# Attention block kernel: kept index weights, no table of factors, and the low parts of absorbed query weights on GpSimd from one staging buffer

## The chip, the cores and the metric

The kernel runs on one core of a Trainium2 chip. The metric is the time of one execution on the device in microseconds (us), as the median over runs. PE is TensorE, ACT is ScalarE, DVE is VectorE, POOL is GpSimd, SP is SyncE, whose queue issues every DMA of this kernel.

## The reference

One transformer block over 1024 rows of 512 numbers. With `xn = layernorm(x)` the result is `x + attention(xn) + experts(xn)`.

```python
q_lat = rmsnorm(xn @ q_a_w); q = q_lat @ q_b_w        # 32 heads, 128 + 64 rotated columns
ckv = xn @ kv_a_w                                      # 64 latent + 64 rotated key columns
kv = rmsnorm(kv_lat) @ kv_b_w                          # keys (128) and values (128) of each head
scores = (q_nope . k_nope + rope(q_pe) . rope(k_pe)) * 192 ** -0.5
iq = (xn @ idx_wq_w)                                   # 16 index heads of 128 columns
idx_scores = sum_n iw[n] * relu(iq[n] . ik)            # a score of each query for each key
mask = top 128 keys of idx_scores, and causal
out = softmax(where(mask, scores, -inf)) @ v @ o_w     # then + low-rank experts, top 2 of 8
```

The choice of the top 128 keys needs nearly full precision, so the kernel splits each float32 operand in a high half in float16 and a low half (the float32 value less the high half, in float16) and takes three products: high-high, high-low, low-high.

## The kernel before

All of the work is one hand-ordered program: each engine has its own list of instructions, and semaphores tie them together. There is no planner; the order of each list is the order of the code.

**Opening** (to about 46 us). Layer norm, transposes of the rows to `xnT` and one projection of 472 columns.

**Index scores, first group** (to about 112 us, `GROUPS[0]`, row tiles 3, 2, 1). For each of 16 index heads `n`, PE's `iq_head(n)` (line 567) multiplies the index weight of that head with `xnT` for rows 128 to 511, and `idx_head` (line 583) multiplies the result with the index keys. The weight comes in float32 by DMA (`load_iq`, line 376) into one of two slots of `wq32`. ACT's `weights` (line 856) copies it to float16 and scales the float32 copy, and POOL's `wq_parts` (line 1364, subtraction at line 1366) makes the low half. Both halves land in one of two slots of `wqp`.

**Index scores, second group** (to about 191 us, `GROUPS[1]`, row tiles 5 and 4; iterations `n` = 0 to 15). PE needs the index queries of rows 512 to 1023, so `iq_head(16 + n)` (matmuls through `indexer`, line 558) wants the same 16 weights again: they are loaded, copied and split a second time, two heads ahead. ACT takes the relu of each bank (line 899) and weighs it (line 876), POOL sums it into `bias` (`join`, line 1432), and DVE meanwhile picks the top 128 of the first group, eight at a time (`top_round`, lines 1182 and 1189). In iterations 3 to 12 PE also transposes normalised rows (line 604), which ACT and DVE copy out. DVE's masks (line 1199) end the group.

**Index scores, third group, and absorbed query weights** (to about 283 us, `GROUPS[2]`, row tiles 7 and 6). In iteration `n` PE does tiles 7 and 6 and `qw_pair(n)` (line 607, matmuls at 614): the product of the latent query weights and the key weights of two heads, 256 columns in `psT`. ACT's list is: relu and weighing of tile 7, relu of tile 6, then four copies of 128 columns to float16 (two from `pe_s`, the rotated columns, two from `psT`, the latent ones; lines 968 to 971) and a scaled copy of `pe_s` in place (line 973). The low halves are split between two engines. DVE makes those of the latent columns straight from PSUM (lines 1221 and 1222), after a top-8 round and the sum of tile 6 (line 1133). POOL makes those of the rotated columns from `pe_s` (`pe_low`, lines 1486 to 1492), after its sum of tile 7. SP loads the operands of pair `p` in three DMAs (`load_qw`, line 391) once both low halves of pair `p - 2` are made. Query units 0 and 1 are also computed, rotated and stored in this stage: after iterations 4 and 9 POOL rotates (`rope_cos`, `rope_sin`, lines 1445 to 1458), and in iterations 6, 8, 12 and 13 it makes one low half each (`q_low`, `rope_low`).

**Attention** (to about 787 us). 32 units (two heads, half of the rows) of 8 steps. A step is scores on PE, row minimum on DVE (line 1242), exponential on ACT, transposes by PE or DMA, the float16 split, and the product with the values. `unit_out` (line 1255) closes a unit on DVE: reciprocal of the row sums, a product of the eight reciprocals with the table `scaled` (line 1260; 1024 for the steps transposed by DMA, 1 for the others), and one multiplication of the whole bank (line 1265).

**Output** (to the end). 48 matmuls a row tile from weights kept in SBUF (line 779), and the rows are stored.

```python
for n in range(IH):                              # DVE, third group
    top_round(GROUPS[1])
    acc(psS[1], 6, n, 3 * IH + n, 5 * IH + 2 * n + 1, 1 if n else 0)
    u = n % 2
    dve.wait_ge(qw_hi, 4 * n + 4)
```

## Time and profile before

| what | value |
|---|---|
| median of 3 runs | 883.79 us (880.57 to 884.02) |
| the profiled execution | 884.29 us |
| its span in the profile | 882.5 us |
| PE busy | 792.2 us, 90% of the span |
| DVE busy | 659.0 us, 75% |
| ACT busy | 583.1 us, 66% |
| POOL busy | 580.6 us, 66% |
| share of the chain that ended last | PE 29%, POOL 26%, DVE 15%, issue 13% |

How to read it: an engine's busy time is a mean over stages that have different limits, so no single share says what bounds the kernel. The span is the time between the first and the last instruction in the profile; the execution's own time is longer by 1.8 us. The chain of waits follows the last instruction back to what released it, step by step.

### The profile page before, as it was taken

Reading aid. Unit: us, or ns where it says so; the run is one execution under the profiler, and the core shown is the slowest. Engines: PE = TensorE matmul, PEld = TensorE weight load, DVE = VectorE, ACT = ScalarE, POOL = GpSimd, SP = SyncE. Lnnn points to the kernel's source line nnn. Section 1 sums busy time; section 2 is a strip of 40 time slices with the busy share of each in tenths; the row PEclk is TensorE's granted clock in tenths of the full one; section 3 lists DMA queues with packets and bytes.
Section 4 is the critical chain, followed back from the end, with each engine's and each line's share of the span. In section 5 each row is a group of like instructions: output and inputs, shape, how many; then the busy total and the mean of one; then the engine's idle time right before and its main releaser. Section 6 shows DMA issues by size and latency. Waiting matters only on the chain.

```text
span 882.5 us, 20077 instructions
## 1 busy us (share of the span) xinstructions
PE 792.2 (90%) x7384; PEld 487.0 (55%) x7384; DVE 659.0 (75%) x1557; ACT 583.1 (66%) x1308; POOL 580.6 (66%) x509
## 2 busy tenths in 40 slices
PE   4979989977776998888888999999999999999998
PEld 2545544434443555555554677776766776764443
DVE  6365677889999999999988888888887888851000
ACT  2656789988886887877877677666666676750000
POOL 3175368876795788878877787887788888740000
PEclk9989999999999999999999999999999999999999
DMA  8012211112343776666676567897777677871110
GB/s 258 25 37 72 72 49 48 49 53 64 109 123 98 153 170 164 174 168 159 169 164 151 111 128 141 154 157 147 138 137 152 131 152 153 165 152 34 52 53 29
DMA packets 198483, 104.00 MB, mean 118 GB/s; under 512 B 146417, under 2 KB 172401, under 8 KB 198385
## 3 DMA queue, kind: packets, MB, share of 16 engines
q1 hardware_dynamic: 198384, 102.72, 51.9%
q8 instruction: 59, 0.97, 0.5%
q14 instruction: 40, 0.32, 0.1%
HBM read 36.62 MB, written 6.29 MB: 49 GB/s over the span
## 4 chain that ended last, share of the span: by engine, by line
PE 29%; POOL 26%; DVE 15%; issue 13%; DMA 7%; SPq 6%; ACT 4%; POOLq 0%; DVEq 0%; ACTq 0%
PE psS L779 9%; DMA arena<-arena 6%; DVE m L1182 4%; SPq L457 4%; PE psS L706 3%; DVE bias L1189 3%; POOL arena L1457 3%; POOL arena L1455 3%; POOL arena L1483 3%; PE psT L578 2%; PE psS L535 2%; DVE arena L1242 2%; PE psT L558 2%; POOL arena L1366 2%; POOL arena L1462 2%
## 5 line engine op out<-in xcount | busy, mean ns | idle before, releaser
L706 PE MATMUL psS<-keyT,arena 128*128 128x512 f16 (+3 forms) x1152 | 231.5, 329 | 14.9 <-DVE small L1242 6.6
L810 ACT ACTIVATE arena<-psT 128x512 f16<-128x512 f32 (+4 forms) x328 | 154.6, 503 | 110.7 <-PE psT L763 65.8
L1242 DVE CUSTOM_DVE_ANT_0 arena<-psS,bias 128x512 f32<-128x512 f32 (+7 forms) x256 | 191.4, 751 | 41.3 <-PE psS L706 17.6
L997 ACT ACTIVATE arena<-arena,small 128x512 f32<-128x512 f32 (+7 forms) x256 | 197.4, 774 | 27.7 <-DVE small L1242 21.1
L1048 DVE SCALAR_TENSOR_TENSOR arena<-psT,arena 128x512 f16<-128x512 f32 (+3 forms) x246 | 126.3, 535 | 23.1 <-ACT arena L810 22.8
L706 PEld LDWEIGHTS psS<-keyT,arena 128*128 128x128 f16 x1152 | 92.6, 98 | 81.2 <-issue 20.7
L591 PE MATMUL psS<-ikT,big 128*128 128x512 f16 (+3 forms) x528 | 103.8, 341 | 24.2 <-DVE bias L1133 20.8
L1432 POOL TENSOR_TENSOR bias<-arena,bias 128x768 f32<-128x768 f32 (+2 forms) x48 | 91.3, 1916 | 32.3 <-ACT arena L876 21.4
L763 PE MATMUL psT<-ident,arena 128*128 128x128 f32 x624 | 97.0, 277 | 10.1 <-DVE arena L1048 6.9
L591 PEld LDWEIGHTS psS<-ikT,big 128*128 128x128 f16 x528 | 49.5, 100 | 73.8 <-DVE bias L1133 28.1
L1189 DVE MATCH_REPLACE8 bias<-m,bias 128x768 f32<-128x768 f32 (+4 forms) x112 | 89.9, 809 | 0.0
L763 PEld LDWEIGHTS psT<-ident,arena 128*128 128x128 f32 x624 | 72.6, 141 | 29.5 <-ACT arena L997 13.8
L1182 DVE MAX8 m<-bias 128x8 f32<-128x768 f32 (+4 forms) x112 | 87.4, 816 | 0.5
L810 ACT ACTIVATE big<-psT 128x512 f16<-128x512 f32 (+1 forms) x64 | 36.3, 568 | 59.5 <-PE psT L742 31.9
L733 PEld LDWEIGHTS psO<-val,arena 128*128 128x128 f16 x1728 | 66.2, 99 | 11.9 <-issue 1.7
L1366 POOL TENSOR_TENSOR arena<-arena 128x512 f16<-128x512 f32 x32 | 37.1, 1161 | 53.9 <-ACT arena L810 53.8
L733 PE MATMUL psO<-val,arena 128*128 128x64 f16 x1728 | 69.5, 194 | 0.5 <-DVE arena L1048 0.2
L1048 DVE SCALAR_TENSOR_TENSOR big<-psT,big 128x512 f16<-128x512 f32 (+1 forms) x64 | 41.9, 655 | 34.4 <-ACT big L810 34.0
L810 ACT ACTIVATE arena<-arena 128x512 f16<-128x512 f32 (+1 forms) x112 | 62.7, 590 | 0.8 <-DMA arena<-in_wiq 0.7
L1455 POOL TENSOR_TENSOR arena<-arena,sq 128x512 f32<-128x512 f32 x32 | 40.8, 1275 | 33.8 <-DMA arena<-arena 33.8
L1483 POOL TENSOR_TENSOR arena<-arena 128x512 f16<-128x512 f32 (+4 forms) x37 | 55.3, 1496 | 3.0
L1133 DVE SCALAR_TENSOR_TENSOR bias<-psS,arena,bias 128x512 f32<-128x512 f32 (+3 forms) x64 | 45.1, 746 | 16.3 <-ACT psS L899 15.8
(164 smaller groups left out, 1417.0 us busy)
## 6 DMA issues: line engine op xcount, KB each, us to landing
arena<-arena SPq DMA_DIRECT2D x192, 128.0 KB, 2.4
arena<-in_wiq SPq DMA_DIRECT2D x32, 256.0 KB, 2.8
arena<-in_ow SPq DMA_DIRECT2D x16, 512.0 KB, 4.1
arena<-in_qbT SPq DMA_DIRECT2D x16, 256.0 KB, 2.5
wvo_parts<-arena SPq DMA_DIRECT2D x16, 256.0 KB, 2.0
arena<-in_qpe SPq DMA_DIRECT2D x16, 128.0 KB, 3.0
arena<-in_x SPq DMA_DIRECT2D x8, 256.0 KB, 3.2
out<-arena SPq DMA_DIRECT2D x8, 256.0 KB, 2.0
```

Of the source, the lines that this page charges most:

```text
L591: last = mm(bank[:, c:c + w], iq[:, a, n, t * P:(t + 1) * P], ikT[:, b, c:c + w], start=(a, b) == (0, 0), stop=(a, b) == (1, 0))
L706: last = mm(bank[:, k:k + w], Q[:, u % 2, h, a, q:q + P], keyT[:, b, h, k:k + w], start=(a, b) == (0, 0), stop=(a, b) == (1, 0))
L733: last = mm(dst, src[:, a, j * P:(j + 1) * P], val[:, b, j, :], start=j == 0 and n == 0, stop=j == nb - 1 and n == 2)
L763: last = nc.tensor.transpose(bank[:, (j % 4) * P:(j % 4 + 1) * P], pr[:, g % 4, j * P:(j + 1) * P], ident[:])
L810: return nc.scalar.activation(dst, src, ACT.Copy, scale=scale)
L997: nc.scalar.activation(pr[:, g % 4, 0:kw], pr[:, g % 4, 0:kw], ACT.Exp, bias=shift[:, g % 4:g % 4 + 1], scale=-1.0, accum_out=rsum[:, unit ...
L1048: return v.scalar_tensor_tensor(out=dst, in0=src, scalar=scale, in1=hi, op0=ALU.mult, op1=ALU.subtract)
L1182: v.max(m8[:, slot], bias[:, TOFF[t]:TOFF[t + 1]]).then_inc(tk_max, 1)
L1189: v.match_replace(out=row, in_to_replace=m8[:, slot], in_values=row, imm_value=TAKEN).then_inc(tk_rep, 1)
L1242: v.tensor_tensor_reduce(out=pr[:, g % 4, 0:kw], in0=bank[:, 0:kw], in1=bias[:, TOFF[t]:TOFF[t + 1]], scale=-c_s, scalar=3e38, op0=ALU.add ...
L1432: g.tensor_tensor(row, src[:, 0:P * (t + 1)], row, ALU.add).then_inc(sum_done, 1)
L1483: g.tensor_tensor(rows_of_turn(d)[:, kw:2 * kw], pr[:, x % 4, 0:kw], rows_of_turn(d)[:, 0:kw], ALU.subtract).then_inc(row_lo, 1)
```

## The change

- **Kept index weights.** `wqp` becomes 16 homes, one for each index head, laid into memory that is free until the third group: `cq` and `sq` (the cosine and sine tables, 4 homes), the arena (5), `w1lo` (4) and `w2s` (3). The second pass of loads, ACT copies and POOL subtractions is gone, and so is PE's wait for it. The tables are loaded after head 19, the first query weights after head 24.
- **No table of factors.** The `scaled` table and its product are gone. `unit_out` multiplies in three instructions in the lower half of the rows and in two in the upper; the one that takes steps transposed by DMA carries the factor 1024.
- **One staging buffer.** `pe_s` gives way to `both`, 256 columns for each of the two operands of a pair: rotated (loaded by DMA, scaled in place) and latent (copied by ACT out of `psT`). ACT then makes each high half in one copy of 256 columns, and POOL's `w_low` each low half in one subtraction of 256 columns. DVE makes none. ACT waits for POOL's low halves of pair `n - 2` before it writes the buffer; PE waits for ACT's copy out of `psT` instead of for DVE.

```diff
-        wqp = view(o + 1024, 4 * HID, F16).rearrange("p (u s k n) -> p u s k n", u=2, s=2, k=KT)
+        wq_homes = ([t[:].bitcast(F16) for t in (cq, sq)] + [view(15488, 3 * 2 * HID, F16), view(o + 1024, 4 * HID, F16)]
+                    + [t[:].rearrange("p a b -> p (a b)") for t in (w1lo, w2s)])
+        wqp = []
+        for home, slots in zip(wq_homes, (2, 2, 3, 2, 4, 3)):
+            wqp += [home[:, 1024 * j:1024 * (j + 1)].rearrange("p (s k n) -> p s k n", s=2, k=KT) for j in range(slots)]
...
-        pe_s = view(15040 + 1280, 2 * 256).rearrange("p (u k n) -> p u k n", u=2, k=2)
+        both = view(16000, 2 * 512).rearrange("p (u k n) -> p u k n", u=2, k=2)
...
-            for i in range(0, IH // 2):
-                load_iq(2 * i, 0, IH, False)
-                load_iq(2 * i + 1, 1, IH, False)
+            sp.wait_ge(iq_mm, IH + 4)
             sp.dma_start(cq[:], cosq).then_inc(ld_cq, 16)
             sp.dma_start(sq[:], sinq).then_inc(ld_cq, 16)
+            sp.wait_ge(iq_mm, IH + 9)
...
             def load_qw(p, u, first):
                 if not first:
-                    sp.wait_ge(qw_lo, 2 * p - 2)
                     sp.wait_ge(pe_lo, 2 * p - 2)
...
             def iq_head(q):
-                u, c = q % 2, q // IH
-                pe.wait_ge(wq_lo, q + 1)
+                u, (c, n) = q % 2, divmod(q, IH)
+                if not c:
+                    pe.wait_ge(wq_lo, n + 1)
...
                 if p >= 2:
-                    pe.wait_ge(qw_lo, 2 * p - 2)
+                    pe.wait_ge(st_sc, 2 * p - 3)
...
-                if q + 2 < 2 * IH:
+                if q + 2 < IH:
                     weights(q + 2, u, False)
...
-                copy(w1hi[:, n, 0:128], pe_s[:, u, 0, :], WQ_S).then_inc(qw_hi, 1)
-                copy(w2s[:, n, 0:128], pe_s[:, u, 1, :], WQ_S).then_inc(qw_hi, 1)
-                copy(w1hi[:, n, 128:256], psT[u][:, 0:128], WQ_S).then_inc(qw_hi, 1)
-                copy(w2s[:, n, 128:256], psT[u][:, 128:256], WQ_S).then_inc(qw_hi, 1)
-                act.wait_ge(qw_hi, 4 * n + 2)
-                copy(pe_s[:, u], pe_s[:, u], WQ_S).then_inc(pe_sc, 1)
+                if n >= 2:
+                    act.wait_ge(pe_lo, 2 * n - 2)
+                copy(both[:, u, :, 128:256], psT[u][:, 0:256].rearrange("p (k n) -> p k n", k=2), WQ_S).then_inc(st_sc, 1)
+                copy(both[:, u, :, 0:128], both[:, u, :, 0:128], WQ_S).then_inc(st_sc, 1)
+                act.wait_ge(st_sc, 2 * n + 2)
+                copy(w1hi[:, n, :], both[:, u, 0, :], 1.0).then_inc(qw_hi, 1)
+                copy(w2s[:, n, :], both[:, u, 1, :], 1.0).then_inc(qw_hi, 1)
...
                 acc(psS[1], 6, n, 3 * IH + n, 5 * IH + 2 * n + 1, 1 if n else 0)
-                u = n % 2
-                dve.wait_ge(qw_hi, 4 * n + 4)
-                low(w1lo[:, n, 128:256], psT[u][:, 0:128], WQ_S, w1hi[:, n, 128:256]).then_inc(qw_lo, 1)
-                low(w2s[64:128, n, 128:256], psT[u][64:128, 128:256], WQ_S, w2s[64:128, n, 128:256]).then_inc(qw_lo, 1)
...
-                dve.wait_ge(ri_done, 2 * u + 1)
-                v.tensor_tensor(rinv, rinv, scaled[:, u // NP], ALU.mult).then_inc(ri_done, 1)
...
-                v.tensor_tensor(op.rearrange("p k (h r) -> p h k r", h=2),
-                                out_bank(u).rearrange("p (h k r) -> p h k r", h=2, k=4),
-                                rinv.rearrange("p (h k) -> p h k", h=2).unsqueeze(3).broadcast_to([P, 2, 4, KVR]),
-                                ALU.mult).then_inc(o_done, 1)
+                step = 4 // len(TURNED[u // NP])
+                v.tensor_tensor(to[:, 0], bank[:, 0], by[:, 0].unsqueeze(2).broadcast_to([P, 4, KVR]), ALU.mult)
+                if step == 2:
+                    v.tensor_tensor(to[:, 1, 1::2], bank[:, 1, 1::2], by[:, 1, 1::2].unsqueeze(2).broadcast_to([P, 2, KVR]), ALU.mult)
+                v.scalar_tensor_tensor(out=to[:, 1, 0::step], in0=bank[:, 1, 0::step], scalar=PR_S,
+                                       in1=by[:, 1, 0::step].unsqueeze(2).broadcast_to([P, 4 // step, KVR]),
+                                       op0=ALU.mult, op1=ALU.mult).then_inc(o_done, 1)
...
-                if IH + n + 2 < 2 * IH:
-                    wq_parts(IH + n + 2, n % 2)
...
-            def pe_low(n):
-                pool.wait_ge(pe_sc, n + 1)
-                g.tensor_tensor(w1lo[:, n, 0:128], pe_s[:, n % 2, 0, :], w1hi[:, n, 0:128], ALU.subtract).then_inc(pe_lo, 1)
+            def w_low(n):
+                pool.wait_ge(qw_hi, 2 * n + 1)
+                g.tensor_tensor(w1lo[:, n, :], both[:, n % 2, 0, :], w1hi[:, n, :], ALU.subtract).then_inc(pe_lo, 1)
+                pool.wait_ge(qw_hi, 2 * n + 2)
                 pool.wait_ge(pe_lo, 2 * n + 1)
-                g.tensor_tensor(w2s[64:128, n, 0:128], pe_s[64:128, n % 2, 1, :], w2s[64:128, n, 0:128],
+                g.tensor_tensor(w2s[64:128, n, :], both[64:128, n % 2, 1, :], w2s[64:128, n, :],
                                 ALU.subtract).then_inc(pe_lo, 1)
```

## Rows read from the trace of the kernel before

**Rows 1.** Windows: stretch, length, busy time of each engine, clock, DMA share, GB/s.
```profile
131.00:191.00 60.00, 55.11 (x310) 28.53 (x309) 47.20 (x122) 55.88 (x86) 50.52 (x34) 1.00 0.19 55
200.00:278.00 78.00, 57.24 (x326) 32.44 (x325) 76.61 (x138) 67.69 (x130) 60.33 (x57) 1.00 0.36 104
340.00:470.00 130.00, 113.61 (x1169) 71.68 (x1167) 122.08 (x350) 104.14 (x297) 103.75 (x102) 0.97 0.68 166
490.00:780.00 290.00, 286.18 (x3739) 203.58 (x3738) 240.46 (x529) 202.65 (x421) 231.96 (x181) 1.00 0.76 145
```
**Rows 2.** Chain of waits, second group: start, us, what.
```profile
164.74 1.17 POOL arena L1366
```
**Rows 3.** Order of time, PE: start, us, line, shapes, count, idle before and releaser.
```profile
112.20 2.75 PE L558 MATMUL psT<-arena 128*128 128x512 f16 x12
...
165.95 2.76 PE L558 MATMUL psT<-arena 128*128 128x512 f16 x12 [0.40 <-POOL arena L1366]
...
170.34 0.61 PE L604 MATMUL psO<-ident,arena 128*128 128x128 f32 x4
...
187.42 2.76 PE L558 MATMUL psT<-arena 128*128 128x512 f16 x12 [0.98 <-POOL arena L1366]
...
237.11 1.00 PE L614 MATMUL psT<-arena 128*128 128x64 f32 x8
```
**Rows 4.** Order of time, ACT, second group.
```profile
163.85 1.14 ACT L810 ACTIVATE arena<-arena 128x512 f16<-128x512 f32 x2
```
**Rows 5.** Order of time, DVE, third group, first and last iterations.
```profile
200.64 1.67 DVE L1182 MAX8 m<-bias 128x8 f32<-128x768 f32 x2
...
276.94 0.28 DVE L1048 SCALAR_TENSOR_TENSOR w1lo<-psT,w1hi 128x128 f16<-128x128 f32 x1
...
277.58 1.69 DVE L1182 MAX8 m<-bias 128x8 f32<-128x768 f32 x2
```
**Rows 6.** Order of time, ACT, third group, iterations 7 and 8.
```profile
238.15 0.31 ACT L810 ACTIVATE w1hi<-arena 128x128 f16<-128x128 f32 x1
...
238.88 0.41 ACT L810 ACTIVATE arena<-arena 128x256 f32<-128x256 f32 x1
...
242.69 0.90 ACT L899 ACTIVATE psS<-psS 128x896 f32<-128x896 f32 x1
```
**Rows 7.** Order of time, POOL, third group, iterations 4 to 6.
```profile
224.97 1.27 POOL L1450 TENSOR_TENSOR arena<-arena,cq 128x512 f32<-128x512 f32 x1
...
228.90 2.36 POOL L1432 TENSOR_TENSOR bias<-arena,bias 128x1024 f32<-128x1024 f32 x1
231.21 0.43 POOL L1488 TENSOR_TENSOR w1lo<-arena,w1hi 128x128 f16<-128x128 f32 x1
231.72 0.42 POOL L1490 TENSOR_TENSOR w2s<-arena,w2s 64x128 f16<-64x128 f32 x1
...
235.54 1.16 POOL L1466 TENSOR_TENSOR arena<-arena 128x512 f16<-128x512 f32 x1
```
**Rows 8.** Order of time, SP's queue, one load of query weights.
```profile
251.88 0.33 SPq L395 DMA_DIRECT2D arena<-in_qbT  x1
...
252.73 0.59 SPq L397 DMA_DIRECT2D arena<-in_qpe  x1
```
**Rows 9.** The page's DMA issues: count, KB each, median us to landing.
```profile
arena<-in_qpe SPq DMA_DIRECT2D x16, 128.0 KB, 3.0
```
**Rows 10.** Line 379 (loads of index weights), all 32.
```profile
DMA to landing us min/median/max: 2.6/2.8/6.3
```
**Rows 11.** Groups by line and shape, DVE, 110 to 205 us: count, busy, mean ns.
```profile
L1199 DVE TENSOR_SCALAR bias<-bias 128x384 f32<-128x384 f32 x1 | 1.7, 1690 | 0.0
...
L1199 DVE TENSOR_SCALAR bias<-bias 128x256 f32<-128x256 f32 x1 | 0.3, 278 | 0.0
```
**Rows 12.** Order of time, DVE, the close of a unit.
```profile
654.40 0.17 DVE L1260 TENSOR_TENSOR small<-small 128x8 f32<-128x8 f32 x1
654.65 0.69 DVE L1265 TENSOR_TENSOR arena<-psO,small 128x512 f32<-128x512 f32 x1
```

More of the change, by code:

```diff
@@ L180, in block_kernel @@
         eps_t = small[:, 400:401]
-        scaled = small[:, 408:424].rearrange("p (c s) -> p c s", c=2)
         nmax_s = small[:, 424:428]
@@ L369, in _, with load_iq @@
             sp.dma_start(bm32, bm).then_inc(ld_c, 16)
+            wiq_v = wiq.rearrange("(k p) n -> p k n", p=P)
+            def load_iq(n, u, first):
+                if not first:
+                    sp.wait_ge(wq_lo, n - 1)
+                sp.dma_start(wq32[:, u], wiq_v[:, :, ds(n * ID, ID)]).then_inc(ld_wq[u], 16)
+            load_iq(0, 0, True)
+            load_iq(1, 1, True)
+            for n in range(2, IH):
+                load_iq(n, n % 2, False)
+            sp.wait_ge(iq_mm, IH + 4)
             sp.dma_start(cq[:], cosq).then_inc(ld_cq, 16)
             sp.dma_start(sq[:], sinq).then_inc(ld_cq, 16)
-            wiq_v = wiq.rearrange("(k p) n -> p k n", p=P)
-            def load_iq(n, u, again, first):
-                if not first:
-                    sp.wait_ge(wq_lo, n + again - 1)
-                sp.dma_start(wq32[:, u], wiq_v[:, :, ds(n * ID, ID)]).then_inc(ld_wq[u], 16)
-            load_iq(0, 0, 0, True)
-            load_iq(1, 1, 0, True)
-            for i in range(1, IH // 2):
-                load_iq(2 * i, 0, 0, False)
-                load_iq(2 * i + 1, 1, 0, False)
-            for i in range(0, IH // 2):
-                load_iq(2 * i, 0, IH, False)
-                load_iq(2 * i + 1, 1, IH, False)
+            sp.wait_ge(iq_mm, IH + 9)
             def load_qw(p, u, first):
                 if not first:
-                    sp.wait_ge(qw_lo, 2 * p - 2)
                     sp.wait_ge(pe_lo, 2 * p - 2)
@@ L396, in load_qw @@
                 sp.dma_start(wk_s[:, u], wkT[:, ds(2 * p, 2), :]).then_inc(ld_qw[u], 16)
-                sp.dma_start(pe_s[:, u].rearrange("p k (h r) -> p k h r", h=2),
+                sp.dma_start(both[:, u, :, 0:128].rearrange("p k (h r) -> p k h r", h=2),
                              qpe[:, :, ds(2 * p, 2), :]).then_inc(ld_qw[u], 16)
@@ L577, in iq_head @@
                     for a, b in ((0, 0), (0, 1), (1, 0)):
-                        last = mm(psT[u][:, 0:CH - P], wqp[:, u, a, k, :], xnT[:, b, k, P:CH],
+                        last = mm(psT[u][:, 0:CH - P], wqp[n][:, a, k, :], xnT[:, b, k, P:CH],
                                   start=ins == 0, stop=ins == 3 * KT - 1)
@@ L1258, in unit_out @@
                 v.reciprocal(rinv, rsum[:, u % 2, :]).then_inc(ri_done, 1)
-                dve.wait_ge(ri_done, 2 * u + 1)
-                v.tensor_tensor(rinv, rinv, scaled[:, u // NP], ALU.mult).then_inc(ri_done, 1)
                 dve.wait_ge(av_mm, UNIT_AV[u])
-                dve.wait_ge(ri_done, 2 * u + 2)
+                dve.wait_ge(ri_done, u + 1)
                 if u:
                     dve.wait_ge(ot_mm, u)
-                v.tensor_tensor(op.rearrange("p k (h r) -> p h k r", h=2),
-                                out_bank(u).rearrange("p (h k r) -> p h k r", h=2, k=4),
-                                rinv.rearrange("p (h k) -> p h k", h=2).unsqueeze(3).broadcast_to([P, 2, 4, KVR]),
-                                ALU.mult).then_inc(o_done, 1)
+                to = op.rearrange("p k (h r) -> p h k r", h=2)
+                bank = out_bank(u).rearrange("p (h k r) -> p h k r", h=2, k=4)
+                by = rinv.rearrange("p (h k) -> p h k", h=2)
+                step = 4 // len(TURNED[u // NP])
[5 more added lines that the diff above has]
+                                       op0=ALU.mult, op1=ALU.mult).then_inc(o_done, 1)
             def ot_low(bank, u):
@@ L1347, in _ @@
             g.memset(eps_t, EPS).then_inc(eps_ok, 1)
-            g.memset(small[:, 408:424], 1.0).then_inc(ones_ok, 1)
-            pool.wait_ge(ones_ok, 1)
-            for c in range(2):
-                for s in TURNED[c]:
-                    at = col_of(s)
-                    ins = g.memset(scaled[:, c, at:at + 1], PR_S)
-            ins.then_inc(eps_ok, 1)
             g.memset(bias[:], 0.0).then_inc(idx_init, 1)
@@ L1421, in _ @@
             gated_rows()
-            for q in range(6, IH + 2):
+            for q in range(6, IH):
                 wq_parts(q, q % 2)
```

23 lines of the change are left out of this document (10 added, 13 removed).

## The prediction

> **What bounds the kernel now.** I read the windows first, to see which engine is full in which stretch, then the chain of waits inside a stretch to see what its end hangs on, then the order of time of one engine for the durations. Four stretches matter [rows 1]. From 131 to 191 us (index heads of row tiles 5 and 4, call it stage D) PE is busy 55.1 of 60 us and ACT 55.9. From 200 to 278 us (tiles 7 and 6, with the absorbed query weights beside them, stage E) DVE is busy 76.6 of 78. In attention, DVE has 122.1 of 130 us in the lower half and PE 286.2 of 290 in the upper.
>
> In stage D the chain steps from GpSimd's subtraction of line 1366, the low part of a reloaded index weight, straight into the head's matmuls [rows 2], and PE shows it as idle time before the head, 0.40 us in a typical iteration [rows 3]. That is the last link of a loop: load, two ACT copies, subtraction, matmul. The two ACT copies alone take 1.14 us [rows 4] on an engine that is otherwise full.
>
> In stage E the DVE iterations follow one another without a gap: the first two maxima start at 200.64 and the sixteenth at 277.58 [rows 5], 76.94 us for 15 iterations, 5.13 each. The loop is rigid because nothing but DVE's own list sets it. Its last 0.64 us of 5.13 (276.94 to 277.58) are the two low parts of lines 1221 and 1222.
>
> **Part 1, kept index weights.** In stage D the change removes 16 loads, 32 ACT copies, 16 POOL subtractions, and PE's wait for them. After that PE has only its own work: from the start of a head to the start of the transposes 4.39 us (165.95 to 170.34), and the transposes take 0.61 us with pipelining, of which I count 0.5 [rows 3]. So 4.89 us in the ten iterations with transposes and 4.39 in the others. From the head that starts at 112.20 to the last one there are 14 steps, ten with transposes and four without: 48.9 + 17.6 = 66.5 us, so the last head starts at 178.7 and not at 187.42. **Gain 8.7 us.** Could another engine take PE's place? ACT falls from about 5.3 us an iteration by 1.14 to some 4.2, POOL from 4.5 to 3.3, DVE has 47.2 busy of 60 us, 4.2 an iteration [rows 1]. All are below 4.89, and below 4.39 by less, so the gain holds, with DVE and ACT next. The tail from the last head to DVE's first maximum of stage E (187.42 to 200.64) is DVE's own two rounds and masks beside POOL's last sums, and moves along whole. Bounds: if ACT or DVE hold every iteration to 5.1 us, 14 x 5.1 = 71.4 gives 3.8; PE's idle time all gone, 9.5.
>
> The moved DMAs: the cosine and sine tables go from the opening to the middle of stage D, where the share of the DMA engines is 0.19 [rows 1]; the first reader is the rotation at 225 us [rows 7], 80 us later. The first loads of query weights wait for head 25, which is also long before stage E. I cost both at nothing; the cover is those tens of us.
>
> **Part 2, the low parts on GpSimd.** DVE loses 0.64 us of each iteration: 16 x 0.64 = 10.2 us, if everyone else can follow a period of 4.50. Here the others come close.
>
> ACT: its small copies and the scaling run from 238.15 to 239.29, 1.14 us [rows 6]. After it are four copies of 128x256; one lasts 0.41 and lets the next start after about 0.3, and the third must wait for the end of the second: 0.3 + 0.4 + 0.05 + 0.3 + 0.3 = 1.35 us. With 2.95 us of other work ACT needs 4.3 of 4.5.
>
> POOL: a sum of 1024 columns occupies it 2.31 us (228.90 to 231.21), a 128x128 low part 0.43 with 0.08 to the next (231.21 to 231.72), a 128x512 one 1.16 [rows 7]. No row shows 128x256; the line between 0.43 and 1.16 gives 0.67, the bounds are 0.43 (as if width were free) and 0.9. I take 0.67, since both neighbours are this same operation. An iteration is then 2.31 + 2 x 0.75 = 3.81 us. On top come two rotations of 3.93 us each (224.97 to 228.90) after iterations 4 and 9, and four subtractions of about 1.12 in iterations 6, 8, 12 and 13: 12.3 us. Sixteen times 3.81 plus 12.3 is 73.3 us, against 16 x 4.50 = 72.0 for DVE. POOL is full, and late after each rotation.
>
> Who waits when POOL is late? One staging buffer (two slots) is freed by POOL alone, and the next-but-one load on SP waits for it. From its low part to the next-but-one copies: three DMAs, the last issued 0.85 us after the first (251.88 to 252.73) and landing 3.0 us later [rows 8, 9], then 1.00 us of PE for the products (row at 237.11) [rows 3], 4.9 us in all. Walk the first rotation in the times of before, stage E still beginning at 200.64. The sum of iteration 4 starts near 202.7 + 4 x 4.5 = 220.7; with its low parts it ends at 224.5, the rotation at 228.5, iteration 5 with its low parts at 232.3. The copies of iteration 7 can start at 237.3, and from the copies of 7 to the relu of iteration 8 ACT needs 4.54 us (238.15 to 242.69) [rows 6]. That relu ends near 242.7, where DVE wants it at 240.4. **2.3 us lost.** The second rotation repeats the pattern with POOL already behind: 2.6 us. Twice more, where ACT also empties a query bank, 0.4. Loss 5.7, so stage E saves 10.2 - 5.7 = **4.5 us**.
>
> GpSimd's low parts were off the chain in iterations; they are 16 x 0.5 us more now. The Trainium skill, "GPSIMD Engine Reference", section 4.1 "Engine selection", speaks against this part: elementwise work with two inputs is about twice as slow there as on VectorE and belongs on VectorE. The rows agree in kind (0.43 against about 0.3 us for 128x128), but by that rule alone one would forecast a loss, while by rows the receiving engine had 18 us idle [rows 1].
>
> The end of stage E: the two masks of tiles 5 and 4 begin while POOL is in its last low parts, which before had ended first. In stage D's tail a mask of 384 columns that overlapped POOL's sums lasted 1.69 us, the one of 256 after them 0.28 [rows 11]. I charge **0.5 us** (bounds 0 and 1.5). The Trainium skill, "SBUF — State Buffer", section "SBUF: two separate sides", states that such a VectorE operation and a GpSimd one hold a shared port exclusively for a whole instruction. This trace agrees; by that rule the charge would reach the 1.5.
>
> **Part 3, no table of factors.** Per unit DVE loses the small product and the wait behind it, 0.25 us (654.40 to 654.65) [rows 12]. The multiplication, 0.69 us, becomes three instructions in the lower half and two in the upper; each further one costs fixed time: the line through 0.28 us for a low part of 128 columns [rows 5] and 0.69 for 512 has 0.14 of it, of which about half overlaps the neighbour, 0.07. Net -0.11 x 16 in the lower half, where DVE is nearly full, and -0.18 x 16 where PE is the bound [rows 1] and it is worth nothing. At most 1.8, and a loss of 0.5 if nothing overlaps; I take **1.0 us**. The memsets at the start lie beside the projections: nothing.
>
> **Sum.** 8.7 + 4.5 - 0.5 + 1.0 = 13.7 us off the profiled execution's 884.29 (span 882.5 and 1.8 around it) gives 870.6. That execution stands 0.5 above the median 883.79, so a median of **870.1 us**. Its own range, by the bounds above, is 866 to 874.
>
> **Rivals.**
> *A. POOL keeps up*, because the 128x256 low part is near 0.5 or loads land faster. Then stage E saves the whole 10.2: 870.1 - 5.7 = 864.4 us. For it: POOL idle 18 us in the stage. Against: the rotations are lumps, and slack before them can't be banked.
> *B. POOL becomes the bound outright.* At 0.9 us a low part an iteration takes 4.27 and the stage 68.3 + 12.3 = 80.6, which with its late start ends where it ends now. Stage E saves 0 to 1: 874 us.
> *C. Stage D gives half*, held by ACT or DVE at 5.1 us an iteration: 870.1 + 4.9 = 875 us. Against: their sums above.
> *D. Nothing to measure*, both stages finding new waits: 882 us, within 0.5%, which is about what a measurement of this kernel tells from no change.
> *E. Slower.* The place is the ring from one low part over SP's load and PE's products to the next-but-one low part: 4.9 + 1.35 + 1.5 = 7.75 us for two iterations, against 9.0. It holds while loads land in 3 us. Were they to land in 6.3 us, the longest landing of an index weight [rows 10], the ring is 11.05, or 5.5 an iteration; sixteen are 88.4, and with POOL's 12.3 lying inside, 100.7 us against 82.1 now: 870.1 + 4.5 + 18.6 = 893 us. It decides from landings of about 5.7 us on. Against: the median of 3.0 in this stage.
>
> **How the numbers follow.** Forecast 0.57, A 0.12, B 0.14, C 0.08, D 0.05, E 0.04. The likeliest gives 870.1. The range takes in A's 864.4 and C's 875 with their own spread, 863 to 878, and leaves out D, E and a little. Faster by over 0.5% (below 879.4): forecast, A, B and C, 0.91. Within: 0.05. Slower: 0.04.
>
> **What would show it.** Stage D: PE's heads 4.9 us apart with no idle time before them, no line 1366 in the chain; a gap of 5.1 or more speaks for C. Stage E: DVE's maxima 4.5 us apart except for two gaps of 6.5 to 7.3 us, near iterations 8 and 13; sixteen even gaps of 4.5 mean A, even gaps near 5 mean B, and PE idle before the products after SP's loads in every iteration E. The 128x256 low part on GpSimd at 0.67 us. Attention unchanged but for about 1 us in the lower half. The forecast is wrong if stage D ends less than 6 us earlier, or stage E takes over 80 or under 73 us.

## The result, and the profile after

The change makes the kernel faster, by less than forecast: 875.42 us as the median of five runs (874.79 to 876.89) against 883.79 (880.57 to 886.68), a ratio of 0.992 with an interval of 0.989 to 0.995. The forecast was 870.1, with a range of 863 to 878.

The profiled execution took 874.79 us, with a span of 872.9. Four marks cut the span: DVE's first maximum of stage E, the first row minimum of attention, and PE's first final product.

| stretch | before, us | after, us | difference | predicted |
|---|---|---|---|---|
| to the first maximum of stage E | 200.64 | 191.20 | -9.44 | -8.7 |
| stage E, to the first row minimum | 83.07 | 83.88 | +0.81 | -4.5 + 0.5 |
| attention, to the final products | 503.16 | 501.95 | -1.21 | -1.0 |
| final products to the end | 95.63 | 95.87 | +0.24 | 0 |

So the whole gain stands in stage D, and the staging buffer, which takes 0.64 us of work off DVE sixteen times, brought nothing. That is what the experiments had to explain.

The page's busy times of the kernel after, and what its chain consists of:

```profile
PE 792.2 (91%) x7384; PEld 487.7 (56%) x7384; DVE 645.0 (74%) x1541; ACT 570.0 (65%) x1260; POOL 569.6 (65%) x486
...
PE 40%; DVE 4%; issue 1%; ACT 0%; DVEq 0%
```

Windows of the kernel after (stretch, length, busy time of PE, PE's weight loads, DVE, ACT and POOL, granted clock, DMA share, GB/s):

```profile
131.00:181.00 50.00, 50.00 (x289) 27.16 (x287) 44.84 (x117) 44.07 (x63) 34.86 (x21) 1.00 0.07 19
191.00:273.00 82.00, 63.56 (x334) 35.35 (x332) 70.44 (x114) 71.26 (x120) 68.51 (x56) 0.93 0.34 99
216.00:222.00 6.00, 4.70 (x26) 2.39 (x24) 5.35 (x9) 5.93 (x11) 5.84 (x5) 1.00 0.27 76
226.60:236.00 9.40, 9.33 (x39) 5.35 (x39) 3.80 (x7) 5.32 (x9) 5.42 (x6) 0.68 0.47 128
256.00:262.00 6.00, 5.93 (x29) 3.80 (x30) 2.76 (x6) 3.66 (x7) 4.85 (x4) 0.72 0.37 99
```

In stage D (131 to 181) PE is busy all of the 50 us; nothing else is near. In stage E (191 to 273) DVE is busy 70.4 of 82 us, where it had been busy 76.6 of 78 [rows 1]: its list is shorter and it now waits. And the granted clock of the whole stage is 0.93 where it was 1.00. Two short stretches carry that fall, 0.68 and 0.72. In them PE is busy nearly all the time and DVE less than half of it. In the 6 us before the first of them (216 to 222) ACT and POOL are busy 5.93 and 5.84 us: there both are full.

Stage D in order of time, PE (start, us, line, shapes, count):

```profile
163.96 2.75 PE L558 MATMUL psT<-arena,w1lo 128*128 128x512 f16 x12
...
168.34 0.61 PE L605 MATMUL psT<-ident,arena 128*128 128x128 f32 x4
168.78 2.75 PE L558 MATMUL psT<-arena,w2s 128*128 128x512 f16 x12
...
177.99 2.75 PE L558 MATMUL psT<-arena,w2s 128*128 128x512 f16 x12
```

The heads are 4.82 us apart (163.96 to 168.78) and no idle time stands before them, where 0.40 and 0.98 stood before [rows 3]. The last head starts at 177.99 instead of 187.42.

Stage E in order of time, DVE (start, us, line, shapes, count, idle before and releaser):

```profile
222.65 1.68 DVE L1182 MAX8 m<-bias 128x8 f32<-128x768 f32 x2
227.01 1.68 DVE L1182 MAX8 m<-bias 128x8 f32<-128x768 f32 x2
236.21 1.15 DVE L1133 SCALAR_TENSOR_TENSOR bias<-psS,arena,bias 128x896 f32<-128x896 f32 x1 [5.81 <-ACT psS L898]
237.28 1.68 DVE L1182 MAX8 m<-bias 128x8 f32<-128x768 f32 x2
...
263.28 1.15 DVE L1133 SCALAR_TENSOR_TENSOR bias<-psS,arena,bias 128x896 f32<-128x896 f32 x1 [4.52 <-ACT psS L898]
```

A normal iteration is 4.36 to 4.37 us (222.65 to 227.01), not 5.13 as in [rows 5]. The next one is 10.27 (227.01 to 237.28), because DVE stands idle 5.81 us before the sum of tile 6. The same happens five iterations on. Over all 15 gaps between maxima the gain is 15 x (5.13 - 4.37) = 11.4 us. Against 4.37 each, the two long gaps give back 5.9 and 4.6 us, three small ones (5.11, 4.99, 4.51) another 1.5. That is 12.0 us, and 77.52 us from first to last maximum instead of 76.94.

DVE names ACT as its releaser. ACT waited for PE's products, and PE's rows tell the rest. First POOL and SP (start, us), then PE:

```profile
217.73 1.27 POOL L1447 TENSOR_TENSOR arena<-arena 128x512 f32<-128x512 f32 x1
219.09 2.36 POOL L1424 TENSOR_TENSOR bias<-arena,bias 128x1024 f32<-128x1024 f32 x1
221.41 0.67 POOL L1478 TENSOR_TENSOR w1lo<-arena,w1hi 128x256 f16<-128x256 f32 x1
222.22 0.67 POOL L1481 TENSOR_TENSOR w2s<-arena,w2s 64x256 f16<-64x256 f32 x1
...
222.92 0.33 SPq L396 DMA_DIRECT2D arena<-in_qbT  x1
...
223.76 0.59 SPq L398 DMA_DIRECT2D arena<-in_qpe  x1
```

```profile
226.67 1.97 PE L615 MATMUL psT<-arena 128*128 128x64 f32 x8 [2.58 <-DMA arena<-in_qpe]
228.43 0.63 PE L624 MATMUL psT<-qlT,w1hi 128*128 128x512 f16 x1
228.86 0.63 PE L625 MATMUL psT<-qlT,w1hi 128*128 128x512 f16 x1
...
230.57 3.64 PE L592 MATMUL psS<-ikT,big 128*128 128x512 f16 x12
234.04 1.00 PE L615 MATMUL psT<-arena 128*128 128x64 f32 x8
...
256.07 1.54 PE L615 MATMUL psT<-arena 128*128 128x64 f32 x8 [3.62 <-DMA arena<-in_qpe]
```

Read it as a relay. POOL's rotation ends at 219.0, its late sum and low parts of pair 5 at 222.89. SP issues the load of pair 7 at 222.92, and the products of pair 7 start at 226.67, after 2.58 us of idle PE. Then comes what the prediction didn't have: the products last 1.97 us where they last 1.00 otherwise (234.04), the 512-column matmuls are 0.43 us apart (228.43 to 228.86), and the clock of the stretch is 0.68. PE has fallen from 2.4 to 1.2 GHz after the idle time, and is back at full speed at about 234 (products of 1.00 us). The Trainium skill, "TensorE: Matmul & The Clock Gate", section "HAM oscillation — how this bites in real kernels", tells of a kernel in which a wait for a DMA drops the clock, so that the work behind the wait starts cold. The rows above agree.

**The theory of load ring and clock:** the staging buffer's gain is given back in two waits of PE for a load that POOL's late low parts release, and a part of each loss, about 2 us, is the clock behind the wait. **The rival of full engines:** POOL or ACT is simply full, and any version with these low parts on POOL takes as long. **The rival of a disturbance:** the shorter stage D or the new memory places disturb stage E, and the buffer alone would gain. For the small term there is the question whether the missing table is worth anything.

### The profile page after: what moved, and what is told of

Same layout as the page of the kernel before. It is cut to its first block and busy times, and to the rows that moved or that the text cites. A ratio compares the mean times of both kernels' runs of the same rounds, so it can differ in the third digit from the quotient of the medians.

```text
span 872.9 us, 19970 instructions
## 1 busy us (share of the span) xinstructions
PE 792.2 (91%) x7384; PEld 487.7 (56%) x7384; DVE 645.0 (74%) x1541; ACT 570.0 (65%) x1260; POOL 569.6 (65%) x486
## 5 line engine op out<-in xcount | busy, mean ns | idle before, releaser
L809 ACT ACTIVATE arena<-psT 128x512 f16<-128x512 f32 (+5 forms) x344 | 160.3, 496 | 114.6 <-PE psT L762 62.7
L1473 POOL TENSOR_TENSOR ikT<-arena,ikT 128x384 f16<-128x384 f32 (+4 forms) x37 | 51.9, 1403 | 3.0
```

Source lines behind the costliest of these rows:

```text
L809: return nc.scalar.activation(dst, src, ACT.Copy, scale=scale)
L1473: g.tensor_tensor(rows_of_turn(d)[:, kw:2 * kw], pr[:, x % 4, 0:kw], rows_of_turn(d)[:, 0:kw], ALU.subtract).then_inc(row_lo, 1)
```

## The experiments

Each run was compared with the kernel before on the same chip, whose own median was 883.0 to 885.0 us; between two runs of small difference the ratio says more than the median. "Stage E" is the time from its first maximum to the first row minimum.

| run | median, us | ratio to before (interval) | first maximum | stage E | to final products | two long gaps |
|---|---|---|---|---|---|---|
| the change | 875.42 | 0.992 (0.989 to 0.995) | 191.20 | 83.88 | 501.95 | 10.27, 8.98 |
| keep_only | 874.54 | 0.989 (0.986 to 0.992) | 190.79 | 83.26 | 500.99 | none |
| stage_only | 885.28 | 1.001 (0.999 to 1.003) | 200.86 | 85.38 | 501.92 | 11.19, 9.60 |
| table_only | 882.85 | 0.998 (0.997 to 1.000) | 200.21 | 83.16 | 501.83 | none |
| fill | 871.80 | 0.985 (0.983 to 0.987) | 191.09 | 81.14 | 499.61 | 8.18, 7.98 |
| three_slots | 869.41 | 0.983 (0.980 to 0.987) | 190.23 | 78.09 | 501.99 | none |
| early_load | 869.16 | 0.983 (0.981 to 0.985) | 190.93 | 80.33 | 500.12 | 6.18, 8.56 |
| early_fill | 869.15 | 0.984 (0.982 to 0.986) | 191.00 | 81.03 | 499.84 | 7.91, 6.99 |
| split_rope | 871.18 | 0.985 (0.983 to 0.986) | 191.25 | 80.87 | 501.48 | 6.22, 9.06 |
| late_low | 869.32 | 0.982 (0.979 to 0.984) | 191.17 | 76.60 | 506.47 | none |
| defer_low | 869.98 | 0.985 (0.983 to 0.986) | 191.41 | 76.51 | 503.36 | none |

The columns behind the ratio are of one profiled execution each, whose own time can lie a few us from its median.

### One part alone

**keep_only** is the kernel after with the old staging and the old table: the kept index weights alone.

```diff
-                copy(both[:, u, :, 128:256], psT[u][:, 0:256].rearrange("p (k n) -> p k n", k=2), WQ_S).then_inc(st_sc, 1)
...
+                copy(w1hi[:, n, 0:128], pe_s[:, u, 0, :], WQ_S).then_inc(qw_hi, 1)
...
+                low(w1lo[:, n, 128:256], psT[u][:, 0:128], WQ_S, w1hi[:, n, 128:256]).then_inc(qw_lo, 1)
+                low(w2s[64:128, n, 128:256], psT[u][64:128, 128:256], WQ_S, w2s[64:128, n, 128:256]).then_inc(qw_lo, 1)
```

> Kept index weights alone: the staging buffer and the split multiplication undone. Theory (the second group gave 9.4 us of the 9.8, the third group nothing): the span falls from 882.5 to 872.5 to 874, the second group's heads stand 4.82 us apart, and the third group takes 82 us with DVE's period at 5.13. Rival (the staging buffer gave its 4.5 us and something else lost them): the span stays above 876.

**stage_only** is the reverse: only the staging buffer, with the second pass of index weights and the table as before. The buffer lies on the index weights' memory, so the first load of query weights waits for the last index head.

```diff
+            sp.wait_ge(iq_mm, 2 * IH)
...
-                if q + 2 < IH:
+                if q + 2 < 2 * IH:
                     weights(q + 2, u, False)
```

> Staging buffer alone: weights reloaded and the table kept; the first loads of query weights start only once the last index head is done, since the memory overlaps. Theory: the third group still takes 81 to 83 us against 82.1, with two long gaps in DVE (about 5.8 and 4.5 us, PE's granted clock below 0.8 after each), and the time is within 1.5 us of before. Rival (the two gaps come from the other parts, the loads of the tables among them): no gaps, 72 to 78 us, some 4 to 8 us faster.

keep_only alone has all of the change's gain: stage E starts at 190.79 and its maxima are 5.13 to 5.14 apart behind the first gap of 5.00, as before the change. Its span, 870.6 us, lies below the 872.5 to 874 expected, because its attention is shorter too (500.99). stage_only has no gain: ratio 1.001. Its maxima are 4.37 apart but for two gaps of 11.19 and 9.60, and 5.11 and 5.03. The clock from 191 to 273 us is 0.90. Here is PE before the first of the two:

```profile
237.64 1.97 PE L613 MATMUL psT<-arena 128*128 128x64 f32 x8 [3.90 <-DMA arena<-in_qpe]
```

The waits and the fall come with the buffer and without the kept weights, so the rival of a disturbance is out.

**table_only** is the kernel before without the table: at the end of a unit, three multiplications (lower half) or two (upper half) instead of one.

```diff
-                dve.wait_ge(ri_done, 2 * u + 1)
-                v.tensor_tensor(rinv, rinv, scaled[:, u // NP], ALU.mult).then_inc(ri_done, 1)
...
+                v.tensor_tensor(to[:, 0], bank[:, 0], by[:, 0].unsqueeze(2).broadcast_to([P, 4, KVR]), ALU.mult)
```

> The table of factors gone and the multiplication split, all else as before. Theory (what the prediction took): 0.11 us a unit in the lower half, 0 to 2 us faster in all, the upper half of attention unchanged; a unit's close on DVE 0.11 us shorter in the lower half and 0.18 in the upper. Rival (it does nothing, and the 1.2 us by which attention was shorter after the change is scatter of attention itself): within 0.5 us, though the close of a unit is shorter.

It is 1.5 us faster (884.38 to 882.85), a ratio of 0.998 (0.997 to 1.000), and attention is 1.3 us shorter in the profile. The close of a unit on DVE, from the reciprocal to the next work, falls from 1.12 us (393.67 to 394.79) to 1.02 (391.56 to 392.58) in the lower half and from 1.09 (654.17 to 655.26) to 0.95 (653.37 to 654.32) in the upper, against 0.11 and 0.18 expected. So the close is shorter, and the term of 1.0 us fits. That the whole time gains nothing isn't excluded by much: the interval ends at 0.9999, and keep_only, which has the table, had a shorter attention still (500.99).

### The load ring and the clock

**fill** is the kernel after with matmuls that nobody reads (22 ahead of PE's wait for pair 7, 30 ahead of that for pair 12), in a part of the bank that is free then. It adds work to PE and takes none of the waits away.

```diff
-                pe.wait_ge(ld_qw[u], 48 * (p // 2) + 48)
...
+                for _ in range({7: 22, 12: 30}.get(p, 0)):
+                    mm(psT[u][:, 256:512], qlT[:, 0, 0:128], qlT[:, 1, 0:256], start=True, stop=True)
+                pe.wait_ge(ld_qw[u], 48 * (p // 2) + 48)
```

> The changed kernel with 22 and 30 matmuls of 256 columns whose result nobody reads, placed on PE just before its waits for the loads of pairs 7 and 12. Theory (each gap is a wait for a load of 2.6 to 3.6 us, and then about 2.5 us more because PE runs at half speed after it): granted clock stays at 1.00 after both waits, the gaps in DVE fall from 5.8 and 4.5 us to about 3.3 and 2.3, the third group from 81.9 to some 77, the time by 4 to 5 us. Rival (GpSimd is full and sets the length; PE's clock only fills time that it would wait anyway): third group within 1 us of 81.9.

PE in order of time, and the window that had a clock of 0.68:

```profile
223.83 2.57 PE L613 MATMUL psT<-qlT 128*128 128x256 f16 x22
...
227.41 1.10 PE L617 MATMUL psT<-arena 128*128 128x64 f32 x8 [1.01 <-DMA arena<-in_qpe]
...
229.43 2.59 PE L592 MATMUL psS<-ikT,big 128*128 128x512 f16 x12
```

```profile
226.60:236.00 9.40, 7.51 (x43) 4.39 (x44) 5.67 (x10) 7.35 (x14) 7.53 (x7) 1.00 0.46 133
```

Added work makes the kernel 3.6 us faster (875.42 to 871.80), somewhat less than the 4 to 5 us expected; measured each against its own runs of the kernel before, the change gains 8.4 us and fill 13.2. PE still waits for the load and its products even start 0.74 us later (227.41 against 226.67), but they take 1.10 us and not 1.97, and the twelve head matmuls 2.59 and not 3.64. The gaps shrink by 2.1 and 1.0 us, and stage E by 2.7. This is the clock's part of the loss, less what the later start costs; the rest of the gap is the wait itself.

**three_slots** gives the staging buffer a third slot and lets SP load the other operands as soon as PE has read the pair before last, so that POOL may be a whole iteration late.

```diff
-        both = view(16000, 2 * 512).rearrange("p (u k n) -> p u k n", u=2, k=2)
+        both = [view(at, 512).rearrange("p (k n) -> p k n", k=2) for at in (16000, 16512, 13312)]
...
-                    sp.wait_ge(pe_lo, 2 * p - 2)
+                    sp.wait_ge(qw_mm, p - 1)
...
+                if p >= 3:
+                    sp.wait_ge(pe_lo, 2 * p - 4)
...
-                if n >= 2:
-                    act.wait_ge(pe_lo, 2 * n - 2)
+                if n >= 3:
+                    act.wait_ge(pe_lo, 2 * n - 4)
```

> The changed kernel with three slots of the staging buffer in place of two, and the loads of the query and key weights started when PE has read the pair before the last, not when GpSimd has made its low parts. GpSimd's work is the same. Theory (the loads come late because a slot waits for GpSimd): PE no longer waits for a load, its clock stays near 1.00, the third group takes 74 to 77 us and the time falls by 5 to 7 us. Rival (GpSimd's own 73 us with what it must wait for set the length): 80 us or more, less than 2 us gained.

Both long gaps are gone. The longest is 5.41, and from the first to the last maximum it is 69.1 us (190.23 to 259.34). The time falls as expected (6.0 us, expected 5 to 7), the stage a little less (78.1, expected 74 to 77). The rival of full engines fails in its strong form: with the same work on POOL and ACT the stage is 5.8 us shorter. But POOL takes over at the end. The last maxima and masks are early, and then DVE waits for POOL's last sum:

```profile
263.70 1.43 DVE L1202 TENSOR_SCALAR bias<-bias 128x768 f32<-128x768 f32 x2
268.32 0.69 DVE L1241 CUSTOM_DVE_ANT_0 arena<-psS,bias 128x512 f32<-128x512 f32 x1 [3.19 <-POOL bias L1427]
```

Behind it PE waits for POOL's last low part (waits of the same kernel from 260 to 300: engine and line, releaser, us in total, times, longest):

```profile
PE psS L708 <- POOL w2s L1484: 4.1, 1, 4.1
```

And behind this wait the clock falls: from 268 to 274 us it is 0.72 here, where early_load (below) has 1.00. The third slot took the falls out of the stage and left one at the start of attention:

```profile
268.00:274.00 6.00, 4.43 (x20) 2.61 (x21) 3.97 (x12) 3.00 (x8) 3.14 (x5) 0.72 0.35 100
```

**early_load** keeps two slots. Only the last of the three DMAs, the one into the staging buffer, still waits for POOL; the other two go once PE has read the pair before last.

```diff
-                    sp.wait_ge(pe_lo, 2 * p - 2)
+                    sp.wait_ge(qw_mm, p - 1)
...
+                if not first:
+                    sp.wait_ge(pe_lo, 2 * p - 2)
                 sp.dma_start(both[:, u, :, 0:128].rearrange("p k (h r) -> p k h r", h=2),
```

> The changed kernel, still two slots; the loads of query and key weights start when PE has read the pair before the last, and only the rotated columns wait for GpSimd's low parts. Theory (a load's way is issue of the two others, 0.85 us, and landing, 3.0; the ring through GpSimd stays): both waits of PE shorten by about 0.85 us but PE's clock still falls after them, the two gaps in DVE go from 5.8 and 4.5 us idle to about 4.6 and 3.4, the third group from 83.9 (first maximum to first row minimum) to 81 to 82. Rival (the order of the loads, not the number of slots, was what three slots repaired): the group falls to below 77.

That takes SP's two earlier issues off the ring, and PE's first wait shrinks from 2.58 to 1.41 us; the second is 2.75. PE in order of time:

```profile
226.17 1.10 PE L617 MATMUL psT<-arena 128*128 128x64 f32 x8 [1.41 <-DMA arena<-in_qpe]
227.11 0.38 PE L626 MATMUL psT<-qlT,w1hi 128*128 128x512 f16 x1
...
228.19 2.59 PE L594 MATMUL psS<-ikT,big 128*128 128x512 f16 x12
...
251.77 1.97 PE L617 MATMUL psT<-arena 128*128 128x64 f32 x8 [2.75 <-DMA arena<-in_qpe]
253.53 4.82 PE L594 MATMUL psS<-ikT,big 128*128 128x512 f16 x12
```

After 1.41 us of idle the clock stayed and the gap is 6.18; after 2.75 it fell, and the gap is 8.56. A fall behind both had been expected; with only one the stage is 80.3 us, below the 81 to 82 expected.

**early_fill** adds 24 unread matmuls to early_load, ahead of the wait for pair 12 alone.

```diff
+                for _ in range({7: 0, 12: 24}.get(p, 0)):
+                    mm(psT[u][:, 256:512], qlT[:, 0, 0:128], qlT[:, 1, 0:256], start=True, stop=True)
```

> The kernel with the earlier loads, plus 24 matmuls of 256 columns whose result nobody reads, on PE just before its wait for the load of pair 12, where PE stood idle 2.75 us and its clock fell. The load itself is untouched. Theory (the fallen clock is a cost of its own beside the wait): granted clock 1.00 after that wait, DVE's gap there 8.56 us from maximum to maximum before, 6.2 to 6.8 now; the other gap (6.18) stays. Rival (the wait alone makes the gap): 8.3 us or more.

At pair 12 the gap goes from 8.56 to 6.99 (6.2 to 6.8 expected) with the clock at 1.00, another 1.6 us of clock. But at pair 7, where the two kernels do the same, this execution fell. PE in order of time, then a window of each kernel, early_fill first:

```profile
226.32 1.08 PE L619 MATMUL psT<-arena 128*128 128x64 f32 x8 [1.48 <-DMA arena<-in_qpe]
227.24 0.49 PE L628 MATMUL psT<-qlT,w1hi 128*128 128x512 f16 x1
227.52 0.63 PE L629 MATMUL psT<-qlT,w1hi 128*128 128x512 f16 x1
...
229.23 3.37 PE L594 MATMUL psS<-ikT,big 128*128 128x512 f16 x12
```

```profile
224.00:240.00 16.00, 12.69 (x64) 6.64 (x62) 12.55 (x21) 13.23 (x23) 14.01 (x12) 0.89 0.42 119
```

```profile
224.00:240.00 16.00, 12.65 (x75) 7.30 (x73) 14.28 (x25) 14.81 (x25) 15.33 (x13) 1.00 0.47 135
```

The idle time is 1.48 us in one and 1.41 in the other. The clock falls in one (0.89) and not in the other (1.00), and the gap is 7.91 instead of 6.18. That is 1.7 us for the clock by itself, with the same work and nearly the same wait: the cleanest reading of it, though no run chose it. One gap was won and one lost in this execution, and the ratio didn't move (0.984, and 0.983 for early_load).

### Easing POOL

**split_rope** moves the sine part of each rotation (three of POOL's instructions in a lump of 3.9 us) one iteration on.

```diff
-                    rope_sin((4, 9).index(n))
+                if n in (5, 10):
+                    rope_sin((5, 10).index(n))
```

> The changed kernel with each rotation of GpSimd cut in two: the cosine part stays after iterations 4 and 9, the sine part and the sum come one iteration later. Same work, same two slots. Theory (it is the lump of 3.9 us that makes the load late by more than the slack): the lumps are 1.2 and 2.7 us, PE's waits for loads become shorter than 1.5 us each, its clock stays at 1.00, and the third group falls by 4 to 7 us to 77 to 80. Rival (the mean of GpSimd's work counts, not its lumps): within 1 us of 83.9.

Stage E is 3.0 us shorter than after the change, but PE still waits, and the clock falls behind both waits, where waits under 1.5 us and a clock of 1.00 had been expected. PE in order of time, then a window behind the first wait:

```profile
231.09 1.10 PE L615 MATMUL psT<-arena 128*128 128x64 f32 x8 [2.33 <-DMA arena<-in_qpe]
232.03 4.24 PE L592 MATMUL psS<-ikT,big 128*128 128x512 f16 x12
...
257.22 1.97 PE L615 MATMUL psT<-arena 128*128 128x64 f32 x8 [3.53 <-DMA arena<-in_qpe]
```

```profile
234.00:236.00 2.00, 2.00 (x7) 0.86 (x5) 1.48 (x3) 1.84 (x2) 1.78 (x4) 0.50 0.29 89
```

Both waits moved an iteration on. The first is 2.33 us long; its products still took 1.10, but about 1 us later the clock fell, to 0.50 from 234 to 236, and the twelve head matmuls took 4.24. The gap there is 6.22 and not 10.27. The second wait is as long as it was (3.53 against 3.62), with the fall and a gap of 9.06. So the lump is a part of the lateness, but not all of it. That the rest is the sum of POOL's work up to that point is my reading, which no run isolates.

**late_low** and **defer_low** both start from three_slots and try to bring POOL's last sum forward. late_low puts the low parts of pair 14 behind the last sum; defer_low puts two low parts of query unit 1 behind everything.

```diff
-                w_low(n)
+                if n < IH - 2:
+                    w_low(n)
+                if n == IH - 1:
+                    w_low(n - 1)
+                    w_low(n)
```

> Three slots, and GpSimd's low parts of pair 14 moved behind its last sum of tile 7. Theory (with three slots GpSimd is the bound, and DVE's first row minimum waits for that sum): the sum ends 1.5 us earlier, the first row minimum comes up to 1.5 us earlier than with three slots alone (268.3), and the time is 0.5 to 1.5 us below. Rival (PE's wait for the last low parts takes its place): no gain.

```diff
-                if n in (6, 12):
-                    q_low((6, 12).index(n))
-                if n in (8, 13):
-                    rope_low((8, 13).index(n))
...
+            q_low(1)
+            rope_low(1)
```

> Three slots, and GpSimd's two low parts of query unit 1 (iterations 12 and 13, 2.3 us) moved behind its last low part of the weights, into the start of attention, where unit 1 is first needed at step 8. Theory (GpSimd's list sets the end of the third group once the slots don't): its last sum ends 2.2 us earlier, the first row minimum comes 1.5 to 2.3 us earlier after the group's start than with three slots (78.1 us from first maximum to first row minimum, so 76 to 76.6), and the time is 1 to 2 us below three slots. Rival (DVE's masks, held up by GpSimd, or PE's wait for the last low parts, take the place as in late_low): 77.5 us or more, no gain.

Both shorten stage E by 1.5 us, and neither gains in the whole. In late_low PE then waits 4.2 us for the low parts that were put last. In defer_low POOL's last sum ends at 266.6 instead of 268.1 and PE's wait is 2.1 instead of 4.1, but DVE's masks now run beside POOL all along (order of time, DVE):

```profile
264.85 3.03 DVE L1202 TENSOR_SCALAR bias<-bias 128x768 f32<-128x768 f32 x2
267.92 0.69 DVE L1241 CUSTOM_DVE_ANT_0 arena<-psS,bias 128x512 f32<-128x512 f32 x1
```

They take 3.03 us where three_slots shows 1.43. What stage E wins, the first steps of attention use up. From the first row minimum to one and the same group of transposes on PE some 12 us later (L764, at 281.17 in three_slots) it is 12.85 us in three_slots, 14.27 in late_low and 15.01 in defer_low, and 11.76 in early_load. Stage E and this stretch together are 90.9, 90.9, 91.5 and 92.1 us. In the three kernels with three slots the clock is 0.72 from 268 to 274 us, and defer_low has a new wait there, 1.83 us of PE for a load of value weights.

## Why the prediction was right or wrong

**Stage D: right, 9.4 instead of 8.7.** PE has no idle time left, as said. The heads are 4.82 us apart and not 4.89, because the transposes add 0.44 (168.34 to 168.78) where I took 0.5. (I had ACT at 5.3 us an iteration before; 55.88 of 60 us [rows 1] at 5.37 us an iteration, (187.42 - 112.20) / 14, is 5.0. It decided nothing.) The other engines stay below PE: ACT 44.1 of 50 us, DVE 44.8, POOL 34.9. Rival C (half the gain) is out. keep_only shows it alone, with the same 50.00 of 50.

**POOL's and ACT's prices: right.** The 128x256 low part on POOL takes 0.67 us, as read from the line between its neighbours, and ACT's four copies 1.32 us (263.19 to 264.51) against 1.35.

**The period: better than forecast.** DVE's iteration is 4.37 and not 4.50. I subtracted the 0.64 us between two starts at the end of the list from 5.13; what went away was 0.76.

**The two gaps: the mechanism and the place right, the size wrong.** The step that failed is "The copies of iteration 7 can start at 237.3, and from the copies of 7 to the relu of iteration 8 ACT needs 4.54 us", from which came the loss of 2.3 us. Measured from the stage's start, the walk down to POOL's low parts was exact: predicted 232.3 - 200.64 = 31.7, measured 222.89 - 191.20 = 31.7. After that the copies were to start at 36.7 and started at 37.5 (228.68), since the products ran at the lower clock (1.97 us, not 1.00). From there to the relu of iteration 8 it took 6.60 us (228.68 to 235.28) and not 4.54. ACT of the change, then of early_load, where the clock held at this place:

```profile
228.68 0.38 ACT L809 ACTIVATE arena<-psT 128x256 f32<-128x256 f32 x1 [3.00 <-PE psT L615]
...
235.28 0.90 ACT L898 ACTIVATE psS<-psS 128x896 f32<-128x896 f32 x1
```

```profile
227.31 0.38 ACT L811 ACTIVATE arena<-psT 128x256 f32<-128x256 f32 x1 [0.97 <-PE psT L617]
...
231.86 0.90 ACT L900 ACTIVATE psS<-psS 128x896 f32<-128x896 f32 x1
```

At full clock the step holds to the hundredth (4.55 us in early_load). It came from a stretch at full clock and isn't valid behind a wait that ends the full clock. The relu came 2.9 us later than forecast, and by rows the clock accounts for it: 0.97 for the products, 5 x 0.21 for the query projection and 1.05 for the head's matmuls (3.64 against 2.59) are 3.1 us on PE. Another 0.6 us of the gap is DVE's shorter period: it stood ready 39.2 us after the stage's start and not 39.8. So the first gap cost 5.9 instead of 2.3, and the second 4.6 instead of 2.6. What fill gave back in the first gap fits: 2.1 us, though its products started 0.85 us later from the stage's start (36.32 against 35.47). With the small gaps the predicted loss of 5.7 us became 12.0. By the signs that the prediction gave, two gaps of 6.5 to 7.3 us and a stage of 73 to 80 us, the forecast of this stage is wrong: the gaps are 10.27 and 8.98, the stage 83.9.

**The end of stage E: within the bounds.** I charged 0.5 us for masks beside POOL, with bounds of 0 and 1.5. Here are the two masks of the kernel after; before the change they took 0.96 us:

```profile
273.08 1.96 DVE L1199 TENSOR_SCALAR bias<-bias 128x768 f32<-128x768 f32 x2
```

They lost 1.0, and POOL's low part beside them was stretched too, 0.99 us instead of 0.67. In defer_low the same two take 3.03. The Trainium skill, "SBUF — State Buffer", section "SBUF: two separate sides", has the two engines shut each other out for a whole instruction. The rows agree, and the price depends on how many of POOL's instructions fall beside the masks.

**The rivals.** A (POOL keeps up) is what three_slots nearly reaches: with a third slot the maxima take 69.1 us, and 15 x 4.37 is 65.6. It has the third slot; with two no run came near it (73.9 us in early_load). B (POOL is the bound outright) is wrong for the change as a whole, where POOL is busy 68.5 of 82 us and stands idle 3.75 us before its next sum at 235.50; but during PE's first wait it was working off its late list, and B is right for what comes behind the change: in three_slots the stage ends with POOL's list. E named the ring that decides and asked landings of 5.7 us of it. They stayed at 3.0, and the waits came from POOL's lateness and not from the DMA.

**The time.** Stage D gave 0.7 more than forecast. Stage E gave 4.8 less (a loss of 0.8 where a gain of 4.5 - 0.5 was forecast), and attention and the end agree within 0.3. The profiled execution was 4.2 us above the forecast for it (874.79 against 870.6), the median 5.3. It lies inside the range (863 to 878) and above the likeliest case's own (866 to 874). So the time came out in range because the range had been widened for the rivals, not because stage E was foreseen: its forecast missed by more than it was worth.

**What stays open.** three_slots, early_load and early_fill, late_low and defer_low lie within a microsecond of 869.4, though their stages E differ by 4.5 us (76.5 to 81.0). Attention takes 499.8 to 506.5 us in their profiles. A part of it is shown (PE's wait for the last low parts, the clock behind it, the masks); why early_load and fill have an attention some 2 us shorter than the change was not settled. It isn't in the first 12 us, which take 11.92 us in the change and 11.76 in both. Nor did a run make one wait longer or shorter by small steps, so what decides whether the clock falls behind a wait of 1.4 to 2.3 us stays unknown.

**The better version.** early_load is a small edit of the change (two waits) and runs at 869.16 us, ratio 0.983 (0.981 to 0.985) to the kernel before, some 6 us below the change. three_slots is as fast (869.41, ratio 0.983).

## What to carry to other kernels

When work moves to an engine with idle time in sum, ask which buffer that engine now frees, and walk one lump of its list through the load behind the buffer. A third slot, or a load that waits only for what it overwrites, may be worth more than the move itself. Where PE would wait for that load, price the wait as its length and the work behind it at half clock, 1.6 to 2.9 us here. And run each part of a change alone: here one part was all of the gain.

## What the runs showed of the hardware

- PE's clock can fall to half behind a single wait in a stage that is otherwise well filled. Behind waits for a load in stage E it fell after idle times of 2.33, 2.58, 2.75, 3.53, 3.62, 3.71 and 3.90 us, and once after 1.48; it held after 1.41 and 1.01. The idle times of up to 1.7 us in which PE waits for DVE, again and again in this stage, did it no harm.
- The last idle time alone doesn't decide. At the start of attention the clock of early_load stayed at 1.00 behind 2.26 us of idle and another 1.06 soon after, while that of the change was 0.55 from 273.3 to 276.5 us, behind 1.36 us; in the 3.3 us before, PE had been busy 1.30.
- Work that nobody reads can pay: 52 matmuls of 256 columns made the kernel 3.6 us faster, by holding the clock over two waits.
- Two masks of 768 columns on DVE take 0.96 us alone, 1.43, 1.96 and 3.03 us beside POOL's sums and subtractions.
